# Layer 1's state from exponentials times the normalised input: two layers of conditioned attention on one core

## The chip, the core and the metric

The kernel runs on one core of a Trainium2 chip. Its engines each work through a list of instructions of their own and wait for each other by semaphores: TensorE (PE: matrix products, with its weight loads shown as PEld), VectorE (DVE), ScalarE (ACT), GpSimd (POOL) and SyncE (SP, which issues most of the transfers). The metric is the device time of one execution in microseconds, the median of several runs.

## What is computed

Two layers work on x of 2 batches x 1024 tokens x 256 channels. Layer 0 is softmax attention over the tokens with 16 heads of 16 channels; layer 1 is linear attention with 8 heads of 32 channels. Layer 1, which the change touches, is:

```
xn = _ln(x, ln_w, ln_b)
q = xn @ Wq + bq
k = xn @ Wk + bk + (1.0 - src_mask) * -1000000.0
q = softmax(q.reshape(b, t, h, dh), axis=-1)
k = softmax(k.reshape(b, t, h, dh), axis=1)
v = ((xn @ Wv + bv) * src_mask).reshape(b, t, h, dh)
att = einsum('bnhd,bnhl->bhdl', k, v)
y = einsum('bnhd,bhdl->bnhl', q, att).reshape(b, t, d)
scale, shift = split((silu(emb) @ W_emb + b_emb)[:, None, :], 2, axis=2)
hh = _ln(y, ln2_w, ln2_b) * (1.0 + scale) + shift
return x + silu(hh) @ W_out + b_out
```

`att` is the state: one 32 x 32 block per head. It is a sum over all tokens, so it needs the keys' softmax of the whole sequence, and every output needs it.

## The kernel before

Tokens are taken in 8 tiles of 128 (`NT`), channels in 2 chunks of 128 (`KC`), halves of 512 tokens (`HALF`). All engines run lists that the Python code fixes ahead.

**The main loop** is 128 steps (`STEPS`) of layer 0's attention: 16 groups (2 batches, 2 halves, 4 groups of 4 heads), each with 8 key tiles. In a step PE computes the scores of 128 keys by 512 queries for 4 heads (`scores`, L986), ACT takes their exponentials (`exponential`, L815), PE multiplies the probabilities of the step before by the values (`values`, L1006), and PE and DVE work ahead on the row maxima of later groups (L876, one product of 512 columns each; L1179, one reduction each). The maxima go round three PSUM banks (`B8[5:8]`) and, in steps that carry a large unit, also borrow banks of the scores (`sT`).

**Everything else is a "unit"**: a piece of PE work that fills one bank, which ACT or DVE then empties. `put` gives units to steps; a unit named in `SMALL` may share a step with another, any other takes a step for itself, and `places` then gives that step 5 maxima in place of 3 (the total of maxima is fixed, so a step that takes fewer leaves them to later steps). PE fills the units at the end of the step (`pe_at`), ACT empties those in `ON_ACT` after its two exponentials, DVE the others. PE waits for a bank until the unit that held it before is emptied.

Layer 1 of batch 0 runs inside the loop, of batch 1 partly. Its units:

- `("T", "in1", b, h, kc)`: `z`, the normalised input before weight and bias, transposed on PE; ACT writes `hT = ln_w * z^T + ln_b` (L904, L738).
- `keys` (L942, bias and mask by DVE, then the maximum and, on ACT, `kexp`: `kE = exp(k - max)` with its sum in `ksum`), `queries` (L851, L853; DVE subtracts the maximum, ACT takes `qexp`, DVE sums in `qsum`), `values` (`by_rows`, L851 twice 2 products and L853 twice a product that adds the bias; ACT writes `v1`, scaled by the mask, L764).
- `kT`: 4 units of 4 transposes of `kE` (L952), copied by ACT to `kN` (L768). `qT`: 4 units (L957, L771).
- `att`, one unit for each 128 channels: 8 products of `kN` by `v1` over the token tiles (L963). DVE scales by the reciprocal of `ksum` and keeps the blocks of the diagonal (L1258).
- `y1` (L970): `qT` by `att`; then the second norm, `T mid1` and `out1`.

A product of two f32 operands shows as two instructions in the trace, a transpose as one.

**The tail** follows the loop: batch 1's second half has its layer 0 output, its `in1` norm, `keys`, `queries` and `values`, and then the state. Its order is written out by hand: `end_order` for PE, `act_end` for ACT, `dve_end` for DVE, with 7 banks taken in turn. `keep_busy` puts products there whose result nobody reads.

`z` has one place per half; the next norm of that half may overwrite it once its last reader is through (L652, L1114). `late` is a shared stretch of memory: `v1` lies where the loop's early part keeps `parts`, the pieces that it stores by DMA.

Of the kernel before, what the change touches and what calls it, by code (L numbers as in the profile page):

```python
# [21 lines left out]
def two_layer_conditioned_attention(  # L22
# [6 lines left out]
    F32, F32R = mybir.dt.float32, mybir.dt.float32r  # L29
# [3 lines left out]
    P = 128  # L33
# [48 lines left out]
    with ctx:  # L82
# [66 lines left out]
        v1 = by_tile(late[:, 2 * TD:3 * TD])  # L149
# [45 lines left out]
        ctanh_ready, tanh_ready = sem("ctanh_ready"), sem("tanh_ready")  # L195
# [11 lines left out]
        ON_ACT = {"T", "v", "values", "kT", "qT", "emb"}  # L207
# [5 lines left out]
        SMALL = {"T", "kT", "qT", "att", "embT", "vec2"}  # L213
# [39 lines left out]
        last = put([("v", 1, s) for s in range(4)], last)  # L253
        for h in range(NH):
# [7 lines left out]
        last = put([("qT", 0, 1, kc) for kc in range(KC)], last)  # L262
        last = put([("att", 0, kc) for kc in range(KC)], last)
# [34 lines left out]
        dve_at[begins["values", 0, 3] + 2].append(("recips", 0))  # L298
# [58 lines left out]


# [28 lines left out]
        end_order += [("queries", b, s) for s in (2, 3)] + [("values", b, s) for s in (2, 3)]  # L387
        end_order += [("qT", b, 0, kc) for kc in range(KC)] + [("kT", b, i) for i in range(4)] + [("qT", b, 1, kc) for kc in range(KC)]
        end_order += [("att", b, kc) for kc in range(KC)] + [("y1", b, s) for s in range(4)]
# [4 lines left out]
        act_end += [("values", b, s) for s in (2, 3)] + [key for key in end_order if key[0] in ("qT", "kT")]  # L394
# [212 lines left out]
        def _(pool):  # L607
# [36 lines left out]
            def normalise(key):  # L644
# [7 lines left out]
                gone = unit[("T", *former, KC - 1)]  # L652
# [43 lines left out]
        def _(act):  # L696
# [11 lines left out]
            def take(key, ending=False):  # L708
# [52 lines left out]
                elif kind == "values":  # L761
# [74 lines left out]
        def _(pe):  # L836
# [19 lines left out]
            def fill(key):  # L856
# [74 lines left out]
                elif kind in ("out0", "out1"):  # L931
                    b, s = key[1:]
                    hT_there("mid0" if kind == "out0" else "mid1", b, s // 2)
                    if kind == "out0" and b == 0 and s == 0:
                        pe.wait_ge(wo_in, 16)
                        pe.wait_ge(w1_in, 16 * 4)
# [6 lines left out]
                elif kind in ("queries", "values"):  # L943
# [392 lines left out]
```

## Time and profile before

| | us |
|---|---|
| median of 3 runs (615.16 to 621.78) | 615.43 |
| the profiled execution | 610.35 |
| its span | 608.5 |
| PE busy, share of the span | 564.3, 93% |
| DVE busy | 450.8, 74% |
| ACT busy | 337.9, 56% |
| POOL busy | 76.5, 13% |

Overview in 40 equal slices of 15.2 us (digits are tenths; PEclk is the granted clock):

```profile
PE   8997989999999999999989999999889999977986
PEld 7454342333543344453334435555335443524765
DVE  6685886887688996878998989759888886314552
ACT  2433454555578754448667575665585566662530
POOL 3010145000000402000010230000422020002200
PEclk9999899999999996999999999999899999999998
```

The loop's first exponentials start at about 59 us and its last ones end at about 542 us; the tail is the rest. The span is read by PE's row: where it shows 9, the loop is paced by PE's list.

### The profile page before, as it was taken

How to read it: one execution, taken by the hardware profiler on the slowest of the kernel's cores; microseconds unless marked ns; L12 is line 12 of the kernel's file. 1: busy time of each engine (PE TensorE's matmuls, PEld its weight loads, DVE VectorE, ACT ScalarE, POOL GpSimd, SP SyncE). 2: the span in 40 equal slices, each digit the busy share in tenths (PEclk: the TensorE clock that was granted, in tenths of full speed). 3: DMA queues.
4: the chain of work that ended last, by engine and by line, in shares of the span. 5: the costliest groups of instructions: out<-in, count | busy, mean ns of one | idle time of the engine just before them, and what ended most of it. 6: DMA issues, size and time to landing. Idle time of an engine off the chain costs nothing. (4 is left out here: it accounts for less than half of the span.)

```text
span 608.5 us, 8404 instructions
## 1 busy us (share of the span) xinstructions
PE 564.3 (93%) x3072; PEld 273.3 (45%) x3072; DVE 450.8 (74%) x915; ACT 337.9 (56%) x410; POOL 76.5 (13%) x126
## 2 busy tenths in 40 slices
PE   8997989999999999999989999999889999977986
PEld 7454342333543344453334435555335443524765
DVE  6685886887688996878998989759888886314552
ACT  2433454555578754448667575665585566662530
POOL 3010145000000402000010230000422020002200
PEclk9999899999999996999999999999899999999998
DMA  5375991356401040404031010010002100000002
GB/s 134 93 155 115 262 236 32 83 141 149 104 27 28 2 81 0 82 0 82 14 69 28 1 28 0 2 53 15 22 2 63 34 2 2 1 0 0 1 2 69
DMA packets 18579, 33.74 MB, mean 55 GB/s; under 512 B 3930, under 2 KB 10450, under 8 KB 17772
## 3 DMA queue, kind: packets, MB, share of 16 engines
q1 hardware_dynamic: 18412, 33.17, 22.3%
q8 instruction: 25, 0.41, 0.3%
q14 instruction: 14, 0.11, 0.1%
q10 hardware_dynamic: 128, 0.04, 0.0%
HBM read 19.29 MB, written 13.52 MB: 54 GB/s over the span
## 5 line engine op out<-in xcount | busy, mean ns | idle before, releaser
L815 ACT ACTIVATE prob<-sT 128x1024 f32<-128x1024 f32 x256 | 247.7, 1023 | 122.9 <-PE sT L986 122.4
L1179 DVE TENSOR_REDUCE halfmax<-bank 128x1 f32<-128x512 f32 x424 | 268.3, 683 | 59.1 <-PE bank L876 57.5
L876 PE MATMUL bank<-ks,qs 50*128 50x512 f32 x424 | 154.3, 481 | 16.0 <-DVE halfmax L1179 8.5
L1006 PE MATMUL bank<-prob,vp 128*17 128x512 f32 x1024 | 136.8, 606 | 0.6 <-ACT prob L815 0.6
L876 PEld LDWEIGHTS bank<-ks,qs 50*128 50x128 f32 x424 | 63.2, 186 | 128.8 <-DVE halfmax L1179 76.6
L986 PE MATMUL sT<-qs,ks 52*128 52x512 f32 x512 | 106.6, 426 | 4.9 <-DMA qs<-crows 2.5
L642 POOL TENSOR_TENSOR rstd<-var,neghalf 128x4 f32<-128x4 f32 x14 | 14.2, 1015 | 483.3 <-DVE var L1103 483.3
L986 PEld LDWEIGHTS sT<-qs,ks 52*128 52x128 f32 x512 | 54.5, 189 | 21.1 <-ACT prob L815 11.3
L1179 DVE TENSOR_REDUCE halfmax<-sT 128x1 f32<-128x512 f32 x88 | 56.8, 685 | 8.0 <-PE sT L876 6.9
L851 PE MATMUL bank<-w,hT 128*128 128x256 f32 x152 | 38.7, 388 | 1.2 <-ACT hT L738 1.2
L1006 PEld LDWEIGHTS bank<-prob,vp 128*17 128x17 f32 x1024 | 17.0, 95 | 40.1 <-issue 37.4
L851 PEld LDWEIGHTS bank<-w,hT 128*128 128x128 f32 x152 | 26.5, 190 | 9.0 <-issue 4.8
L876 PEld LDWEIGHTS sT<-ks,qs 50*128 50x128 f32 x88 | 8.2, 183 | 37.5 <-ACT prob L815 37.5
L667 POOL TENSOR_TENSOR xs<-xs,bias_rows 128x256 f32<-128x256 f32 x32 | 23.3, 728 | 7.2 <-DMA bias_rows<-in_L_cond_b_out 3.2
L876 PE MATMUL sT<-ks,qs 50*128 50x512 f32 x88 | 22.0, 495 | 0.4 <-ACT prob L815 0.4
L911 PE MATMUL bank<-hT,wqk 128*128 128x512 f32 x36 | 19.3, 662 | 0.2 <-DVE halfmax L1179 0.2
L904 PE MATMUL bank<-ident,z 128*128 128x128 f32 x96 | 15.3, 295 | 4.3 <-DVE z L1120 2.4
L1199 DVE RECIPROCAL rden<-bank 128x16 f32<-128x16 f32 x16 | 4.0, 251 | 19.9 <-PE bank L899 19.9
L745 ACT ACTIVATE late<-bank,cols 128x512 fp32r<-128x512 f32 x9 | 6.2, 687 | 21.4 <-PE bank L911 21.4
L738 ACT ACTIVATE hT<-bank,cols 128x512 f32<-128x512 f32 x12 | 8.9, 774 | 14.8 <-PE bank L904 14.6
L853 PE MATMUL bank<-brow,ones 128*128 128x256 f32 x36 | 16.8, 468 | 0.0
L738 ACT ACTIVATE hT<-bank,modB,modA 128x512 f32<-128x512 f32 x12 | 9.1, 776 | 13.6 <-PE bank L904 13.2
(169 smaller groups left out, 541.8 us busy)
## 6 DMA issues: line engine op xcount, KB each, us to landing
stack_rows<-late SPq DMA_DIRECT2D x12, 512.0 KB, 6.7
qs<-stack_rows SPq DMA_DIRECT2D x30, 192.0 KB, 3.5
ks<-stack_rows SPq DMA_DIRECT2D x14, 384.0 KB
stack_rows<-late SPq DMA_DIRECT2D x17, 256.0 KB, 5.6
out_x<-xs SPq DMA_DIRECT2D x4, 512.0 KB, 2.9
xs<-in_x SPq DMA_DIRECT2D x4, 256.0 KB, 3.4
xs<-in_x SPq DMA_DIRECT2D x2, 512.0 KB, 4.0
late<-in_L_cond_emb_w SPq DMA_DIRECT2D x1, 1024.0 KB, 9.8
```

The costliest lines, as they stand in the source:

```text
L642: pool.tensor_tensor(rstd[:, L, :], var[:, L, :], neghalf[:, :], op=ALU.pow).then_inc(pow_ready, 1)
L667: pool.tensor_tensor(xs[:, t, :], xs[:, t, :], bias_rows[:, row, :], op=ALU.add).then_inc(biased, 1)
L738: act.activation(hT[:, kc, h * HALF:(h + 1) * HALF], u.bank, func, scale=scale, bias=bias).then_inc(u.done, 1)
L815: act.activation(prob[:, c % 2, 2 * u:2 * u + 2, :].rearrange("p j n -> p (j n)"), sT[u][:, :], ACT.Exp).then_inc(exp_done, 1)
L851: last = pe.matmul(o[:, i * D:(i + 1) * D], hT[:, kc, tokens], w[:, kc, :], start=(kc == 0), stop=(kc == KC - 1 and row is None))
L853: last = pe.matmul(o[:, i * D:(i + 1) * D], ones[:, :], brow[:, row, :], start=False, stop=True)
L876: last = pe.matmul(o, qs[rows, s % SLOTS, c, t * P:(t + 1) * P], ks[rows, hg, c, half * HALF:(half + 1) * HALF], start=True, stop=True)
L904: last = pe.transpose(o[:, i * P:(i + 1) * P], z[:, h * QT + i, kc * P:(kc + 1) * P], ident[:, :])
L911: last = pe.matmul(o, wqk[:, kc, hg, :], hT[:, kc, n * HALF:(n + 1) * HALF], start=(kc == 0), stop=(kc == KC - 1))
L986: last = pe.matmul(sT[u][:, two * HALF:(two + 1) * HALF], ks[rows, hg, u, c * P:(c + 1) * P], qs[rows, s % SLOTS, u, :], start=True, stop= ...
L1006: last = pe.matmul(acc[32 * j:32 * j + VW, :], vp[:, b, c, hg * GH + j, :], prob[:, c % 2, 2 * u + two, :], start=(c == 0), stop=(c == NT ...
L1179: dve.tensor_reduce(halfmax[:, s % 2, r, half:half + 1], o, axis=AX.X, op=ALU.max, negate=True).then_inc(u.done, 1)
```

## The change

The state is written another way. With E the keys' exponentials and `xn = ln_w * z + ln_b`, the sum over tokens of E times (xn @ Wv + bv) is (E^T z) scaled by `ln_w`, times Wv, plus a rank-one term: the column sums of E times the row `ln_b @ Wv + bv`. So:

- The `values` units go (4 a batch: 6 in the loop, 2 in the tail), and `v1` with them.
- New `kz` units, 2 a batch: for each 128 channels of `z`, 8 products over the token tiles with `z` as weights and 256 columns of `kN` moving; ACT writes them out scaled by `ln_w`.
- A new unit `bvb`, once, in step 26: the row `ln_b @ Wv + bv` on all partitions, copied by ACT after a wait for the last of `parts`' stores.
- `kT` is emptied with the mask as scale, in two ACT instructions of 256 columns where there was one of 512.
- `att` becomes 8 products of `kN` by one column of ones (the column sums), then 2 products of `kz` by Wv. DVE takes three chained instructions for it where it took one.
- In the tail the keys are transposed ahead of the queries, on PE and ACT; ACT empties `kz` ahead of the second half's `qT`.
- `z` is now also read by `kz`: the norm that overwrites it waits for that (`z_read`).

```diff
-        v1 = by_tile(late[:, 2 * TD:3 * TD])
+        kz = late[:, 2 * TD:2 * TD + KC * D].rearrange("p (k n) -> p k n", k=KC)
+        bvb = late[:, 2 * TD + KC * D:2 * TD + (KC + 1) * D]
+        att_sum = late[:, 2 * TD + (KC + 1) * D:2 * TD + (KC + 2) * D].rearrange("p (k n) -> p k n", k=KC)
...
-            first = put([("queries", b, 2 * h + i) for i in range(2)], first)
-            return put([("values", b, 2 * h + i) for i in range(2)], first)
+            return put([("queries", b, 2 * h + i) for i in range(2)], first)
...
+        put([("bvb",)], last + 2)
...
+        last = put([("kz", 0, kc) for kc in range(KC)], last)
         last = put([("att", 0, kc) for kc in range(KC)], last)
...
+        def z_read(key):
+            return unit["kz", key[1], KC - 1] if key[0] == "in1" else unit[("T", *key, KC - 1)]
...
-        act_end += [("values", b, s) for s in (2, 3)] + [key for key in end_order if key[0] in ("qT", "kT")]
+        act_end += [("kT", b, i) for i in range(4)] + [("qT", b, 0, kc) for kc in range(KC)]
+        act_end += [("kz", b, kc) for kc in range(KC)] + [("qT", b, 1, kc) for kc in range(KC)]
...
+                elif kind == "kz":
+                    act.activation(kz[:, key[2], :], u.bank[:, 0:D], ACT.Copy, scale=col("ln_w", key[2])).then_inc(u.done, 1)
+                elif kind == "kT":
                     for i in range(2):
                         t = 2 * key[2] + i
-                        last = act.activation(v1[:, t, :], u.bank[:, i * D:(i + 1) * D], ACT.Copy, scale=col("mask1", b * NT + t))
+                        last = act.activation(kN[:, t, :], u.bank[:, i * D:(i + 1) * D], ACT.Copy, scale=col("mask1", b * NT + t))
...
+                elif kind == "bvb":
+                    pe.wait_ge(w1_in, 16 * 4)
+                    pe.wait_ge(cols_ready, 2)
+                    for kc in range(KC):
+                        c = COL["ln_b"] + kc
+                        pe.matmul(o[:, 0:D], cols[:, c:c + 1].to_broadcast([P, P]), w1[:, 2, kc, :], start=(kc == 0), stop=False)
+                    last = pe.matmul(o[:, 0:D], ones[:, :], brow[:, 2, :], start=False, stop=True)
...
                     for t in range(NT):
-                        last = pe.matmul(o[:, 0:P], kN[:, t, kc * P:(kc + 1) * P], v1[:, t, kc * P:(kc + 1) * P], start=(t == 0), stop=(t == NT - 1))
+                        pe.matmul(o[:, P:P + 1], kN[:, t, chunk], ones[:, 0:1].bitcast(F32), start=(t == 0), stop=(t == NT - 1))
+                    pe.wait_ge(unit["kz", b, KC - 1].done, unit["kz", b, KC - 1].done_at)
+                    for i in range(KC):
+                        last = pe.matmul(o[:, 0:P], kz[:, i, chunk], w1[:, 2, i, chunk], start=(i == 0), stop=(i == KC - 1))
+                elif kind == "kz":
+                    b, kc = key[1:]
+                    for t in range(NT):
...
+                        last = pe.matmul(o[:, 0:D], z[:, t, kc * P:(kc + 1) * P], kN[:, t, :], start=(t == 0), stop=(t == NT - 1))
...
+                    dve.tensor_copy(ksum[:, b, kc:kc + 1], o[:, P:P + 1]).then_inc(ks_ready, 1)
+                    dve.wait_ge(ks_ready, 2 * (KC * b + kc) + 1)
+                    dve.scalar_tensor_tensor(out=att_sum[:, kc, :], in0=bvb[:, kc * P:(kc + 1) * P], scalar=ksum[:, b, kc:kc + 1], in1=o[:, 0:P],
+                                             op0=ALU.mult, op1=ALU.add).then_inc(ks_ready, 1)
+                    dve.wait_ge(ks_ready, 2 * (KC * b + kc) + 2)
+                    dve.scalar_tensor_tensor(out=att[:, b, kc, :], in0=att_sum[:, kc, :], scalar=rksum[:, b, kc:kc + 1], in1=blocks[:, :],
                                              op0=ALU.mult, op1=ALU.mult).then_inc(u.done, 1)
```

PE's list of the tail, from the last two products of `queries` of the kernel before (first two lines) over `values`, `qT` (L957), `kT` (L952) and `att` (L963) to `y1` (L970):

```order
L851 MATMUL sT<-w,hT 128x256 x2
L853 MATMUL sT<-brow,ones 128x256
...
L851 MATMUL bank<-w,hT 128x256 x2
L853 MATMUL bank<-brow,ones 128x256
L957 MATMUL bank<-ident,late 128x128 x8
L952 MATMUL sT<-ident,late 128x128 x16
L957 MATMUL bank<-ident,late 128x128 x8
L963 MATMUL bank<-late 128x128 x8
L963 MATMUL sT<-late 128x128 x8
L970 MATMUL sT<-att,late 128x128 x12
```

and now the same stretch behind `queries`: `kT` (L970), `qT` (L975), `kz` (L990), and for each of the two `att` units the ones (L980) and Wv (L983), then `y1` (L997):

```order
L970 MATMUL sT<-ident,late 128x128 x4
L970 MATMUL bank<-ident,late 128x128 x12
L975 MATMUL sT<-ident,late 128x128 x16
L990 MATMUL bank<-late,z 128x256 x16
L980 MATMUL bank<-ones,late 128x1 x8
L983 MATMUL bank<-w,late 128x128 x2
L980 MATMUL sT<-ones,late 128x1 x8
L983 MATMUL sT<-w,late 128x128 x2
L997 MATMUL sT<-att,late 128x128 x12
```

What moved: the four `values` groups and the 16 products of `att` are gone, all transposes stand together, and `kz` stands between them and the state.

PE's list in the loop where batch 0's state is made, before (steps 88 to 91; L876 are maxima, L986 scores, L1006 probabilities times values, L899 an output's transposes, L957 `qT`, L963 `att`):

```order
L957 MATMUL bank<-ident,late 128x128 x8
L876 MATMUL bank<-ks,qs 128x512 x2
L986 MATMUL sT<-qs,ks 128x512 x4
L1006 MATMUL bank<-prob,vp 17x512 x4
L876 MATMUL bank<-ks,qs 128x512
L899 MATMUL bank<-ident,yT 128x128 x4
L963 MATMUL bank<-late 128x128 x8
L876 MATMUL bank<-ks,qs 128x512 x2
L986 MATMUL sT<-qs,ks 128x512 x4
L876 MATMUL bank<-ks,qs 128x512
L1006 MATMUL bank<-prob,vp 17x512 x4
L963 MATMUL bank<-late 128x128 x8
```

and now, from the second `kz` unit (L990) of step 89 to the end of step 90 (the same operations are L889, L1013, L1033, L912 here):

```order
L889 MATMUL sT<-ks,qs 128x512 x2
L912 MATMUL bank<-ident,yT 128x128 x4
L990 MATMUL bank<-late,z 128x256 x8
L889 MATMUL bank<-ks,qs 128x512 x2
L1013 MATMUL sT<-qs,ks 128x512 x4
L1033 MATMUL bank<-prob,vp 17x512 x4
L889 MATMUL bank<-ks,qs 128x512
L980 MATMUL bank<-ones,late 128x1 x8
L983 MATMUL bank<-w,late 128x128 x2
L980 MATMUL bank<-ones,late 128x1 x8
L983 MATMUL bank<-w,late 128x128 x2
```

What moved: steps 88 and 89 carry one `kz` unit each, and both `att` units stand in step 90, where each had a step of its own. Between steps 50 and 90 these plans changed, no other: `values` left steps 51, 52, 83 and 84 (whose maxima went from 5 to 3), steps 58 and 59 went from 3 maxima to 5, so did 88 and 89, and the transposes moved up by one to three steps. Steps 121 and 122 lost their `values` units and carry no maxima in either kernel.

## Rows read from the trace of the kernel before

**Rows 1.** Page, busy time; and a window of 50 us (columns: stretch, length, busy, clock, DMA)

```profile
PE 564.3 (93%) x3072; PEld 273.3 (45%) x3072; DVE 450.8 (74%) x915; ACT 337.9 (56%) x410; POOL 76.5 (13%) x126
300.00:350.00 50.00, 45.46 (x273) 19.39 (x273) 45.08 (x93) 31.10 (x35) 7.41 (x13) 1.00 0.15 34
```

**Rows 2.** Timeline of ACT, steps 51 to 54 (start, us, instruction, idle before)

```profile
263.64 1.94 ACT L815 ACTIVATE prob<-sT 128x1024 f32<-128x1024 f32 x2 [3.12 <-PE sT L986]
...
269.28 1.94 ACT L815 ACTIVATE prob<-sT 128x1024 f32<-128x1024 f32 x2
...
274.28 1.94 ACT L815 ACTIVATE prob<-sT 128x1024 f32<-128x1024 f32 x2
276.64 1.94 ACT L815 ACTIVATE prob<-sT 128x1024 f32<-128x1024 f32 x2 [0.42 <-PE sT L986]
```

**Rows 3.** Timeline of PE at the start of step 51

```profile
264.45 0.50 PE L876 MATMUL bank<-ks,qs 50*128 50x512 f32 x1 [0.61 <-DVE late L1250]
```

**Rows 4.** Timeline of ACT, a step with 5 maxima and no unit

```profile
292.39 1.94 ACT L815 ACTIVATE prob<-sT 128x1024 f32<-128x1024 f32 x2 [0.52 <-PE sT L986]
296.03 1.94 ACT L815 ACTIVATE prob<-sT 128x1024 f32<-128x1024 f32 x2 [1.70 <-PE sT L986]
```

**Rows 5.** Timeline of ACT, steps 89 to 91: the two that carried `att`

```profile
400.42 1.94 ACT L815 ACTIVATE prob<-sT 128x1024 f32<-128x1024 f32 x2 [0.34 <-PE sT L986]
405.10 1.94 ACT L815 ACTIVATE prob<-sT 128x1024 f32<-128x1024 f32 x2 [2.74 <-PE sT L986]
409.19 1.94 ACT L815 ACTIVATE prob<-sT 128x1024 f32<-128x1024 f32 x2 [2.16 <-PE sT L986]
```

**Rows 6.** Timeline of ACT, steps 121 to 123, which carry no maxima

```profile
523.23 1.94 ACT L815 ACTIVATE prob<-sT 128x1024 f32<-128x1024 f32 x2 [0.87 <-PE sT L986]
...
527.73 1.94 ACT L815 ACTIVATE prob<-sT 128x1024 f32<-128x1024 f32 x2
...
531.53 3.77 ACT L815 ACTIVATE prob<-sT 128x1024 f32<-128x1024 f32 x4
```

**Rows 7.** The chain that ended last: `queries`' last bias, `values`' first products (start, us)

```profile
571.43 0.12 PE sT L853
571.55 0.86 PE sT L851 x4
```

**Rows 8.** Timeline of PE in the tail

```profile
576.18 1.91 PE L952 MATMUL sT<-ident,late 128*128 128x128 f32 x16
...
579.37 2.02 PE L963 MATMUL bank<-late 128*128 128x128 f32 x16 [0.40 <-ACT late L768]
581.22 1.95 PE L963 MATMUL sT<-late 128*128 128x128 f32 x16
583.71 2.92 PE L970 MATMUL sT<-att,late 128*128 128x128 f32 x24 [0.54 <-DVE att L1258]
```

**Rows 9.** Timeline of ACT in the tail: the first `values` unit emptied

```profile
573.63 0.82 ACT L764 ACTIVATE late<-sT,cols 128x256 f32<-128x256 f32 x2
```

**Rows 10.** Timeline of DVE: the one instruction of the state in the tail

```profile
583.21 0.35 DVE L1258 SCALAR_TENSOR_TENSOR att<-sT,rksum,blocks 128x128 f32<-128x128 f32 x1 [1.44 <-PE sT L963]
```

**Rows 11.** Two lines' instructions: f32 products of one moving column; transposes of two

```profile
L1025 PE MATMUL bank<-ident,late x12: 245/245/266, 6.2 to 7.5; 1*128 1x1 f32 x12
L930 PE MATMUL bank<-ident,late x8: 196/197/218, 115.0 to 115.4; 2*128 2x2 f32 x8
```

**Rows 12.** Windows of the tail (columns as in rows 1; the clock is third from the end)

```profile
560.00:562.00 2.00, 1.09 (x8) 0.86 (x8) 0.00 (x0) 1.27 (x2) 1.73 (x3) 1.00 0.00 0
...
564.00:566.00 2.00, 2.00 (x4) 0.89 (x3) 0.11 (x1) 0.00 (x0) 1.76 (x4) 0.54 0.00 0
...
576.00:578.00 2.00, 2.00 (x21) 2.00 (x19) 0.00 (x0) 2.00 (x5) 0.00 (x0) 1.00 0.00 0
```

**Rows 13.** Timeline of PE in the tail: `keys`, 4 instructions at a lower clock, then 4

```profile
562.23 3.62 PE L942 MATMUL bank<-hT,w 128*128 128x512 f32 x4 [1.10 <-ACT hT L738]
565.64 1.98 PE L942 MATMUL sT<-hT,w 128*128 128x512 f32 x4
```

More of the change, by code:

```diff
@@ L204, in two_layer_conditioned_attention @@
         stack_rows = nc.dram_tensor("stack_rows", [G, P, PIECES, T], F32, kind="Internal").ap()
-        ON_ACT = {"T", "v", "values", "kT", "qT", "emb"}
+        ON_ACT = {"T", "v", "bvb", "kz", "kT", "qT", "emb"}
         stream = [("max", s, m) for s in range(SUBS) for m in range(MAXES)]
-        SMALL = {"T", "kT", "qT", "att", "embT", "vec2"}
+        SMALL = {"T", "kT", "qT", "att", "embT", "vec2", "bvb"}
         at = {}
@@ L297, in two_layer_conditioned_attention @@
             dve_mid[2 * h + 2].append(("aggr", "in0", 1, h))
-        dve_at[begins["values", 0, 3] + 2].append(("recips", 0))
+        dve_at[begins["queries", 0, 3] + 3].append(("recips", 0))
         for (kind, b, h), k in layer_at.items():
@@ L386, in two_layer_conditioned_attention @@
         end_order += [("T", "in1", b, 1, kc) for kc in range(KC)] + [("keys", b, 1, kc) for kc in range(KC)]
-        end_order += [("queries", b, s) for s in (2, 3)] + [("values", b, s) for s in (2, 3)]
-        end_order += [("qT", b, 0, kc) for kc in range(KC)] + [("kT", b, i) for i in range(4)] + [("qT", b, 1, kc) for kc in range(KC)]
-        end_order += [("att", b, kc) for kc in range(KC)] + [("y1", b, s) for s in range(4)]
+        end_order += [("queries", b, s) for s in (2, 3)]
+        end_order += [("kT", b, i) for i in range(4)] + [("qT", b, 0, kc) for kc in range(KC)] + [("qT", b, 1, kc) for kc in range(KC)]
+        end_order += [("kz", b, kc) for kc in range(KC)] + [("att", b, kc) for kc in range(KC)] + [("y1", b, s) for s in range(4)]
         for h in range(NH):
@@ L942, in fill @@
                         last = pe.matmul(o, w1[:, 1, k, kc * P:(kc + 1) * P], hT[:, k, n * HALF:(n + 1) * HALF], start=(k == 0), stop=(k == KC - 1))
-                elif kind in ("queries", "values"):
-                    b, s = key[1:]
-                    last = by_rows(o, w1[:, 0] if kind == "queries" else w1[:, 2], s, 1 if kind == "queries" else 2)
+                elif kind == "queries":
+                    last = by_rows(o, w1[:, 0], key[2], 1)
+                elif kind == "bvb":
+                    pe.wait_ge(w1_in, 16 * 4)
[4 more added lines that the diff above has]
+                    last = pe.matmul(o[:, 0:D], ones[:, :], brow[:, 2, :], start=False, stop=True)
                 elif kind == "kT":
@@ L1257, in take @@
                         dve.wait_ge(blocks_ready, 1 + P // DH1)
-                    dve.scalar_tensor_tensor(out=att[:, b, kc, :], in0=o[:, 0:P], scalar=rksum[:, b, kc:kc + 1], in1=blocks[:, :],
+                    if b == 0 and kc == 0:
+                        there = unit["bvb",]
+                        dve.wait_ge(there.done, there.done_at)
+                    dve.tensor_copy(ksum[:, b, kc:kc + 1], o[:, P:P + 1]).then_inc(ks_ready, 1)
[4 more added lines that the diff above has]
+                    dve.scalar_tensor_tensor(out=att[:, b, kc, :], in0=att_sum[:, kc, :], scalar=rksum[:, b, kc:kc + 1], in1=blocks[:, :],
                                              op0=ALU.mult, op1=ALU.mult).then_inc(u.done, 1)
```

20 lines of the change are left out of this document (10 added, 10 removed).

## The prediction

> **What bounds the kernel now.** I read the page first, for busy time: PE is busy 564.3 of 608.5 us and no other engine over 451 [rows 1]. Shares are means, so the timelines come next. In the loop one step lasts from one pair of exponentials (ACT, L815) to the next, and ACT, idle before most of them, waits there for PE's scores. Step 53, which carries nothing but 3 maxima, lasts 276.64 - 274.28 = 2.36 us; step 52, with a `values` unit and 5 maxima, 274.28 - 269.28 = 5.00; step 51 before it, the same but behind `queries`, 269.28 - 263.64 = 5.64 [rows 2]. Where a step has 5 maxima and no unit, the step lasts 296.03 - 292.39 = 3.64 and ACT idles 1.70 of it [rows 4]; DVE, which must reduce them, is busy 45.1 of the 50 us that follow soon after [rows 1]. So PE's list paces steps with units, and DVE's those where postponed maxima are made up. Without maxima ACT is the bound: in step 123 and 124 four exponentials take 3.77, or 1.88 a step [rows 6]. In the tail the timelines of PE, ACT and DVE show one chain: `queries`, `values`, transposes, `att`, DVE's scaling, `y1` [rows 7, 8, 10]. All that is changed lies on PE's list or on this chain, so I cost it place by place.
>
> **The prices.** Two f32 products of 256 columns, four instructions, take 0.86 us and the bias product 0.12 [rows 7], so a `values` unit, twice that, is 1.96, and one f32 product of 256 columns is 0.43. A `kz` unit is 8 such products, 3.44. Sixteen instructions of `att`, 128 columns wide, take 581.22 - 579.37 = 1.85 [rows 8], 0.115 each, and so 8 old products are 1.85 and the 2 new ones with Wv 0.46. A transpose is at most 1.91 / 16 = 0.12 [rows 8]; the last one's latency is in that, so I take 0.11 in a row.
>
> **The ones.** 8 products by one column are 16 instructions, each with 128 columns of weights to load. What is their pitch? The nearest row is an f32 product of 128 weight columns by one moving column: 12 in 7.5 - 6.2 = 1.3 us, eleven spacings, 0.118 each. The other side is the transposes with two moving columns, 8 in 0.4, 0.057 each; they are single instructions, not pairs [rows 11]. I take 0.112, between the first and the 0.115 of `att`, for the operand types and the pairs of instructions are those of the first. The ones then cost 1.79 a unit, what the 128-column products cost: shrinking the moving side buys nothing where the weights have to be loaded anyway. `att` is 2.25 a unit in place of 1.85. At 0.057 it would be 1.37.
> The Trainium skill, page TensorE: Matmul & The Clock Gate, section Back-to-back issue gap, gives 1 to 64 moving columns a gap of about 25 ns; by that the ones would be 0.4 us a unit, an estimate from the page, and the whole sum 5.6 us lower. The products of the startup, at 0.118 [rows 11], contradict it for this form.
>
> **bvb, step 26.** Two 256-column products and a bias product, 0.99, in a step that PE paces, its eviction behind ACT's exponentials, the transfers it waits for long landed: **+1.0**. Fully hidden would be 0.
>
> **Steps 51 to 59.** The two `values` units go. Step 52 falls from 5.00 to a quiet 2.36: -2.64. Step 51 falls less far, since DVE has `queries` in hand until 264.45 [rows 3]: from there 0.43 for the probabilities' start (264.88), 0.85 for them, two maxima and scores, 0.85, and the exponentials begin near 266.8, 3.2 after 263.64: -2.4. The two `qT` transposes only change steps. Steps 58 and 59 now take 5 maxima: 2 x (3.64 - 2.36) = +2.6, DVE-bound. Sum **-2.5**. Bounds: PE's own saving, 2 x 1.96 = -3.9; and 0 if DVE takes all.
>
> **Steps 83 to 90.** Again -5.0 for the two `values` steps (same pattern, half 1). A `kz` step is a `values` step with 3.44 in place of 1.96, 6.48, against the quiet 2.36: +4.1, twice, 8.2. The `att` units cost 2 x 2.25 in place of 2 x 1.85, +0.8 (before, the two steps took 4.68 and 4.09 [rows 5]). ACT empties `kT` in two instructions of about 0.41 (two take 0.82 [rows 9]), beside exponentials of 1.94 in steps of 3.5, +0.2. DVE's three instructions follow while PE goes on with maxima: 0. Sum **+4.2**. By PE's list alone, with the old `att` as cover for nothing: -3.9 + 6.9 + 0.8 = +3.8.
>
> **Steps 121 and 122.** They last 527.73 - 523.23 = 4.50 and 3.80 [rows 6]. Without the unit ACT paces them: 1.88, and in 121 the queries' exponential, 0.6, on top: 2.5 and 1.95. Sum **-3.8**. Nothing is postponed here.
>
> **The tail.** `queries` ends at 571.55 [rows 7]. Before, `y1` began at 583.71 [rows 8]. Now:
> - 8 units of transposes on PE. `kT` takes 1.75. ACT comes to it only when the queries' exponentials are through, 573.63 [rows 9], and empties eight pieces of 0.41: 576.9. The fourth `qT` unit needs the bank of `kT` 0 (emptied 574.45) and ends at 574.9; the first `kz` needs the bank of `kT` 1, 575.3.
> - `kz`: 575.35 + 6.88 = 582.2. Its last tiles want `kT` 3 (576.9) at 577.9: no wait.
> - The ones of `att` 0, 1.79, cover ACT's emptying of `kz` 1 (0.45); Wv 0.46; `att` 1 2.25: 586.7.
> - DVE: a copy of one column, not in the trace, costs between nothing and the 0.35 of a 128-column instruction: I take 0.2; two instructions of 0.35 [rows 10], two more waits of about 0.04, and the 0.15 from the old one's end, 583.56, to `y1` at 583.71: 1.14 behind the last product where 0.52 stood. `y1` at 587.8. The second half's `qT` is emptied by ACT at 583.7, in time.
>
> **+4.1**, and what follows `y1` is unchanged.
>
> **Sum.** 1.0 - 2.5 + 4.2 - 3.8 + 4.1 = +3.0 on the profiled 610.35, whose span is 608.5. The runs' median, 615.43, lies 5.1 above the profiled one; I put the sum on it: **618.4 us**. Batch by batch: the loop's PE work falls, but `kz` gathers for the whole sequence after the keys, so what was spread over both halves' steps lands behind the wait in the tail.
>
> **Clock.** The granted clock falls to half after thin stretches: PE busy 1.09 of 2 us in 560 to 562, 0.54 granted in 564 to 566 [rows 12], and the first four instructions of `keys` take 3.62 where the next four take 1.98, less 0.2 of the last one's latency [rows 13]: +1.84 for one such stretch. The tail now has 3.5 us of nothing but transposes, then 1.79 of one-column products twice and 1.1 of idleness. Transposes alone are harmless: 576 to 578 has nothing else and is granted 1.00 [rows 12].
> The Trainium skill (TensorE: Matmul & The Clock Gate, Part 4: PE-mode transpose) says that transposes do not count as PE being busy. By that the clock should have fallen in this stretch, and `kz` would now begin at 1.2 GHz; rival 5 has the price. The row of 576 to 578 does not bear it out.
> No row shows a run of one-column products near other work.
>
> **Rivals.**
> 1. *The ones are cheap* (pitch 0.057): 32 of them a batch save 1.76, twice 3.5: **614.9**. For: the transposes of two columns. Against: the startup's products at 0.118. The 25 ns of the Trainium skill (same page and section as above) would put this rival further down still.
> 2. *The ones starve the clock*: PE counts as idle in them, and one stretch at 1.2 GHz, the lower level, follows in the loop (step 90 or 91) and one in the tail (`y1`): 2 x 1.84, **622.1**, slower than before by 1.1%. One stretch alone gives 620.2 and decides nothing; the second decides. For: 1.79 + 0.46 + 1.79 + 0.46 + 1.1 us thinly filled. Against: the tail's `att` unit before kept 1.00, and the loads of weights run on.
> 3. *DVE takes it all in steps 51 to 59*: postponed maxima cost what `values` saved: **620.9**. For: 45.1 of 50 us busy.
> 4. *The made-up maxima find gaps*: the steps made up cost only PE's price, 0.43 for two of them, and DVE fits them in: -3.9 + 0.9 in place of -2.5: **617.9**, and 617.0 if they are free.
> 5. *The transposes starve the clock*: one stretch at 1.2 GHz at the tail's first `kz`, 1.84: **620.2**. Against: 1.00 granted in 576 to 578 [rows 12]. The Trainium skill's rule on transposes, named above, is what speaks for it.
>
> **How the numbers follow.** Forecast 0.48; rival 1 0.14; rival 2 0.13; rival 3 0.10; rival 4 0.09; rival 5 0.03; something that I don't see 0.03. A change under 1%, 6.2 us, can hardly be told from none here (the three runs alone span 6.6). Forecast and rivals 1, 3, 4 and 5 lie within it: 0.84. Slower is rival 2, 0.13; faster by 1% would need 609.3, 9 us under the sum, and gets what I don't see: 0.03. The range goes from just under rival 1 to rival 2: 614 to 622.2; more than two low stretches, and more than one term off at once, are left out. The likeliest case's own range is 616.5 to 620.5.
>
> **What would show it.** `kz` units of about 3.5 us each; the ones of one unit in 1.8; steps 121 and 122 at 2.5 and 1.95; steps 88 and 89 near 6.5; from the end of `queries` to `y1` 16.3 us where 12.2 stood; the clock at 1.00 behind the ones. The prediction fails if the ones' pitch is half of what I took, if the clock falls with them, or if runs of the new kernel fall into low-clock stretches elsewhere.

## The result and the profile after

The changed kernel takes 628.0 us (median of 5 runs, 622.5 to 630.3) where the kernel before took 619.7 beside it: ratio 1.021, 95% interval 1.015 to 1.027. The forecast was 618.4 with a range to 622.2 and 0.84 on "within 1%"; the time lies above the range, on the side that had 0.13. Ratios here leave disturbed runs out, so they need not be the quotient of the medians.

The profiled execution is the fastest, 622.48 us with a span of 620.5, against 610.35 and 608.5 before. Its page: busy time and the rows of PE and of the granted clock in 40 slices:

```profile
PE 575.1 (93%) x3077; PEld 281.2 (45%) x3077; DVE 451.8 (73%) x923; ACT 336.1 (54%) x407; POOL 76.5 (12%) x126
PE   8997899999999999999989999999899999987985
PEclk9999858999999999999999799999899999999979
```

PE is busy 10.8 us more than in [rows 1], though its instructions are as many (3077 against 3072) and the share is still 93%. The clock row shows where at least part of that is: slices with 5, 7 and 7, and two with 8, where the kernel before has 9.

**The steps, as predicted or not.** First the chip's state aside: ACT at steps 51 and 52, whose `values` units went (columns: start, us, instruction, idle before and for whom):

```profile
269.58 1.94 ACT L828 ACTIVATE prob<-sT 128x1024 f32<-128x1024 f32 x2 [3.13 <-PE sT L1013]
271.41 0.63 ACT L738 ACTIVATE late<-late 128x512 f32<-128x512 f32 x1
272.57 1.94 ACT L828 ACTIVATE prob<-sT 128x1024 f32<-128x1024 f32 x2 [0.53 <-PE sT L1013]
274.80 1.09 ACT L784 ACTIVATE late<-bank 128x512 f32<-128x512 f32 x2 [0.29 <-PE bank L975]
276.22 3.00 ACT L828 ACTIVATE prob<-sT 128x1024 f32<-128x1024 f32 x3 [0.34 <-PE sT L1013]
```

Step 51 is 272.57 - 269.58 = 2.99 us (5.64 in [rows 2]), step 52 is 276.22 - 272.57 = 3.65 (5.00). The two `qT` evictions, 1.09 us of ACT, now stand in step 52 between exponentials, but ACT still waits for PE's scores behind them (0.34): PE has the `qT` transposes in this step:

```profile
274.11 1.09 PE L975 MATMUL bank<-ident,late 128*128 128x128 f32 x8
```

In steps 121 and 122 ACT alone is left:

```profile
535.83 1.94 ACT L828 ACTIVATE prob<-sT 128x1024 f32<-128x1024 f32 x2 [0.87 <-PE sT L1013]
537.65 0.63 ACT L738 ACTIVATE late<-late 128x512 f32<-128x512 f32 x1
538.17 3.77 ACT L828 ACTIVATE prob<-sT 128x1024 f32<-128x1024 f32 x4
```

From 535.83 to 538.17 are 2.34 us (4.50 in [rows 6]). The four exponentials behind it are steps 122 and 123 back to back; 122 had 3.80 before. The tail, on PE, from the end of `queries` (578.14) to `y1` (L997):

```profile
578.14 0.60 PE L970 MATMUL sT<-ident,late 128*128 128x128 f32 x4
578.57 1.47 PE L970 MATMUL bank<-ident,late 128*128 128x128 f32 x12
579.88 2.03 PE L975 MATMUL sT<-ident,late 128*128 128x128 f32 x16
581.98 7.17 PE L990 MATMUL bank<-late,z 128*128 128x256 f32 x32
588.99 1.84 PE L980 MATMUL bank<-ones,late 128*128 128x1 f32 x16
590.70 0.69 PE L983 MATMUL bank<-w,late 128*128 128x128 f32 x4
591.22 2.20 PE L980 MATMUL sT<-ones,late 128*128 128x1 f32 x16
593.28 1.20 PE L983 MATMUL sT<-w,late 128*128 128x128 f32 x4
595.59 1.62 PE L997 MATMUL sT<-att,late 128*128 128x128 f32 x6 [1.11 <-DVE att L1293]
```

The two `kz` units take 7.17 us, 3.59 each. The first 16 instructions of ones take 1.84, 588.99 to the products with Wv at 590.70 less a latency, a pitch near 0.11. The second 16 take 2.20 and the four products behind them 1.20 instead of 0.69: the clock fell within them. DVE's three instructions, behind the last product (columns as before):

```profile
594.52 0.16 DVE L1288 COPY ksum<-sT 128x1 f32<-128x1 f32 x1 [2.17 <-PE sT L983]
594.71 0.35 DVE L1290 SCALAR_TENSOR_TENSOR late<-late,ksum,sT 128x128 f32<-128x128 f32 x1
595.10 0.35 DVE L1293 SCALAR_TENSOR_TENSOR att<-late,rksum,blocks 128x128 f32<-128x128 f32 x1
```

That is 595.59 - 594.52 = 1.07 us, against 1.14 predicted. Windows of the same execution (columns as in [rows 1]; the third from the end is the granted clock): the loop over and behind its ones (413.65 to 418.3), the tail over its first 16 instructions of ones and over the second 16 with what follows them, and one stretch in steps 76 and 77, which the change does not touch:

```profile
412.00:418.00 6.00, 6.00 (x52) 4.67 (x49) 2.71 (x6) 1.94 (x2) 0.00 (x0) 1.00 0.00 1
418.00:422.00 4.00, 4.00 (x21) 1.36 (x19) 2.71 (x6) 1.94 (x2) 0.00 (x0) 0.57 0.40 131
589.00:592.00 3.00, 3.00 (x29) 3.00 (x27) 0.51 (x2) 2.73 (x4) 0.00 (x0) 1.00 0.00 0
592.00:596.00 4.00, 2.89 (x16) 2.62 (x16) 1.21 (x4) 0.00 (x0) 0.00 (x0) 0.57 0.00 0
350.00:355.00 5.00, 4.64 (x21) 1.67 (x24) 3.77 (x7) 1.60 (x3) 4.52 (x9) 0.52 0.00 0
```

Both places with ones end in a stretch near the lower level of 1.2 GHz. Steps 76 and 77 lie in one too, where the kernel before has 1.00.

**The account by stages.** Differences to the profile of the kernel before, from the starts of ACT's exponentials. In brackets: us at the lower clock in that stage, this kernel / the kernel before. Two further columns are kernels of the experiments: all ones 128 columns wide, and no ones at all with `bvb` in step 67.

| stage | predicted | changed kernel | ones 128 wide | no ones, bvb in step 67 |
|---|---|---|---|---|
| start and steps 0 to 25, same lists | 0 | +8.3 (20.5 / 3.4) | +7.3 (23.9) | +4.7 (6.8) |
| step 26 (`bvb`) | +1.0 | +1.2 | +1.2 | 0 |
| steps 27 to 50, same lists | 0 | -3.5 (0 / 10.2) | +1.9 (13.7) | -3.5 (0) |
| steps 51 to 61 | -2.5 | -2.5 | -2.5 | -2.5 |
| steps 62 to 82, same lists (last column: and `bvb`) | 0 | +2.7 (6.8 / 0) | +2.7 (6.8) | +3.5 (6.8) |
| steps 83 to 92 | +4.2 | +5.4 (3.4 / 0) | +4.2 (0) | +0.5 (0) |
| steps 93 to 120, same lists | 0 | +1.1 (6.8 / 3.4) | +1.3 (6.8) | +1.3 (6.8) |
| steps 121 to 127 | -3.8 | -4.1 | -4.1 | -4.1 |
| tail | +4.1 | +3.6 (7.5 / 8.5) | +1.0 (0.5) | -1.8 (1.0) |

Where no stretch at the lower clock lies in or beside a step, all kernels with the same list in it give it the same length within 0.04 us, but for nine steps (31, 39, 55, 60, 68, 123 to 126), which differ by up to 0.34. So the rows of "same lists" are clock.

### The profile page after: what moved, and what is told of

Read it like the earlier page. It is cut to its first block and busy times, and to the rows that moved or that the text cites. A ratio compares the mean times of both kernels' runs of the same rounds, so it can differ in the third digit from the quotient of the medians.

```text
span 620.5 us, 8422 instructions
## 1 busy us (share of the span) xinstructions
PE 575.1 (93%) x3077; PEld 281.2 (45%) x3077; DVE 451.8 (73%) x923; ACT 336.1 (54%) x407; POOL 76.5 (12%) x126
## 5 line engine op out<-in xcount | busy, mean ns | idle before, releaser
L889 PE MATMUL bank<-ks,qs 50*128 50x512 f32 x428 | 157.3, 489 | 16.8 <-DVE halfmax L1206 9.3
L1033 PE MATMUL bank<-prob,vp 128*17 128x512 f32 x1024 | 140.5, 622 | 0.3 <-ACT prob L828 0.3
L889 PEld LDWEIGHTS bank<-ks,qs 50*128 50x128 f32 x428 | 64.7, 189 | 133.6 <-DVE halfmax L1206 77.4
L1013 PE MATMUL sT<-qs,ks 52*128 52x512 f32 x512 | 109.0, 433 | 5.9 <-DMA qs<-crows 3.5
L1013 PEld LDWEIGHTS sT<-qs,ks 52*128 52x128 f32 x512 | 55.6, 191 | 23.2 <-ACT prob L828 12.4
L1206 DVE TENSOR_REDUCE halfmax<-sT 128x1 f32<-128x512 f32 x84 | 54.0, 684 | 8.5 <-PE sT L889 7.9
L1033 PEld LDWEIGHTS bank<-prob,vp 128*17 128x17 f32 x1024 | 17.1, 96 | 40.8 <-issue 38.3
L864 PE MATMUL bank<-w,hT 128*128 128x256 f32 x96 | 24.1, 388 | 1.2 <-ACT hT L748 1.2
L889 PEld LDWEIGHTS sT<-ks,qs 50*128 50x128 f32 x84 | 7.8, 183 | 36.5 <-ACT prob L828 36.5
L889 PE MATMUL sT<-ks,qs 50*128 50x512 f32 x84 | 21.2, 501 | 0.5 <-ACT prob L828 0.5
L864 PEld LDWEIGHTS bank<-w,hT 128*128 128x128 f32 x96 | 16.9, 190 | 6.3 <-issue 3.0
L917 PEld LDWEIGHTS bank<-ident,z 128*128 128x128 f32 x96 | 11.6, 154 | 10.2 <-DVE halfmax L1206 4.3
```

The costliest lines, as they stand in the source:

```text
L864: last = pe.matmul(o[:, i * D:(i + 1) * D], hT[:, kc, tokens], w[:, kc, :], start=(kc == 0), stop=(kc == KC - 1 and row is None))
L889: last = pe.matmul(o, qs[rows, s % SLOTS, c, t * P:(t + 1) * P], ks[rows, hg, c, half * HALF:(half + 1) * HALF], start=True, stop=True)
L917: last = pe.transpose(o[:, i * P:(i + 1) * P], z[:, h * QT + i, kc * P:(kc + 1) * P], ident[:, :])
L1013: last = pe.matmul(sT[u][:, two * HALF:(two + 1) * HALF], ks[rows, hg, u, c * P:(c + 1) * P], qs[rows, s % SLOTS, u, :], start=True, stop= ...
L1033: last = pe.matmul(acc[32 * j:32 * j + VW, :], vp[:, b, c, hg * GH + j, :], prob[:, c % 2, 2 * u + two, :], start=(c == 0), stop=(c == NT ...
L1206: dve.tensor_reduce(halfmax[:, s % 2, r, half:half + 1], o, axis=AX.X, op=ALU.max, negate=True).then_inc(u.done, 1)
```

## The experiments

**The kernels themselves again.** The spread from run to run had to be known first; neither kernel has an edit.

> The kernel before, once more, to have the granted clock and the span of each of its runs beside those of the changed kernel. The profile after showed 12.0 us more in the span, of which 8.3 lie before step 26, where both kernels run the same list: 2.7 in the first 15 us, where the clock rose later, and 4.9 in steps 3 to 6, where 17 us were granted at half. Theory A (chance): the place and number of the low-clock stretches vary from run to run in either kernel, so this kernel too shows such runs: a profile with another set of stretches than 61, 231 to 241, 436, 562 and 593, runs between 610 and 622, mean granted clock between 0.955 and 0.98. Theory B (the change brings them): this kernel stays at 0.97 to 0.98 in all runs, and the same stretches as in the first profile come back.

> The changed kernel once more. The steps and the tail that the change touches account for +3.5 us in the profiles: +1.2, -2.5, +5.4, -4.1, +3.6. Theory A: the ratio to the kernel before comes down to 1.004 to 1.010, and its runs overlap with those of the kernel before; the stretches behind the ones (418 and 592) may come back or not. Theory B: the ratio stays at 1.015 to 1.025, and the mean granted clock stays 0.01 to 0.02 under that of the kernel before.

Measured: the kernel before again 617.0 us (611.2 to 623.3, 12 runs), ratio 1.005 (1.001 to 1.009), though nothing was changed: a ratio within 0.5% means nothing here. Its profile repeats that of the kernel before, low stretches included, within 0.6 us. The runs differ with their mean granted clock: 611.2 us at 0.979, 616.96 at 0.963, 623.28 at 0.955, about 4 us per 0.01. So each theory was half right: the runs spread as Theory A has it, the profile repeated as Theory B has it. The changed kernel again: 622.8 us (621.3 to 629.5, 6 runs) beside 614.05 (23 runs), ratio 1.019 (1.014 to 1.023); mean clock 0.960 against 0.971. At 4 us per 0.01 the clock is 4.4 of the 8.8 us between the medians. This is Theory B of the second text: the difference stayed. In its profile, which has a span of 627.6, the clock stays low for longer behind the ones of the loop:

```profile
418.00:423.00 5.00, 5.00 (x25) 2.32 (x24) 2.75 (x6) 1.94 (x2) 0.00 (x0) 0.58 0.33 105
423.00:429.00 6.00, 6.00 (x25) 3.12 (x25) 3.96 (x6) 1.94 (x2) 0.00 (x0) 0.50 0.00 0
```

**Ones 128 columns wide.** The same weights and the same number of products, with more for the array to do.

```diff
-pe.matmul(o[:, P:P + 1], kN[:, t, chunk], ones[:, 0:1].bitcast(F32), ...)
+pe.matmul(o[:, P:2 * P], kN[:, t, chunk], ones[:, 0:P].bitcast(F32), ...)
```

> The changed kernel, but the column sums are taken with 128 moving columns of ones in place of one (the 127 further columns of the result are not read). If the pitch of 0.112 us comes from loading 128 f32 weight columns, a product with 128 moving columns costs as much: 16 instructions in 1.8 us, units and steps as long as before. If the ones starve the clock (the stretches at 418 and 592 to 599 begin just behind them), filling the array's moving side takes both stretches away: 1.2 us less in step 91 and 2 to 2.5 less around y1 in the tail, 3 to 4 us in all. If the clock fell there by chance or for the wait of 1.1 us behind them, nothing changes.

Measured: 619.5 us (617.4 to 623.3, 6 runs), ratio 1.012 (1.008 to 1.016). Steps 83 to 92 are +4.2, as forecast, and the whole is 3.3 us under the narrow form. Windows over and behind the ones of the loop, and over and behind those of the tail:

```profile
418.00:422.00 4.00, 4.00 (x36) 3.94 (x36) 1.55 (x4) 0.47 (x1) 0.00 (x0) 1.00 0.00 2
422.00:426.00 4.00, 3.87 (x28) 1.93 (x27) 2.89 (x7) 1.94 (x2) 0.00 (x0) 1.00 0.37 131
592.00:597.00 5.00, 4.99 (x43) 4.75 (x41) 0.86 (x3) 2.73 (x4) 0.00 (x0) 1.00 0.00 0
597.00:601.00 4.00, 2.90 (x26) 2.93 (x27) 2.39 (x6) 0.00 (x0) 0.00 (x0) 1.00 0.02 4
```

The clock is 1.00 throughout. The tail's first transposes (the end of `queries`) and its `y1` on PE:

```profile
581.50 0.60 PE L970 MATMUL sT<-ident,late 128*128 128x128 f32 x4
...
598.10 2.13 PE L997 MATMUL sT<-att,late 128*128 128x128 f32 x17 [1.11 <-DVE att L1293]
```

16.6 us between them at full clock, where 16.3 were forecast and 17.45 stand in the changed kernel.

**No ones.** `att` is the product over `kz` with Wv, times the reciprocal of the keys' sum, plus `bvb`: DVE needs no sum from PE, and two instructions instead of three.

```diff
-for t in range(NT):
-    pe.matmul(o[:, P:P + 1], kN[:, t, chunk], ones[:, 0:1].bitcast(F32), ...)
-dve.tensor_copy(ksum[...], o[:, P:P + 1])
-dve.scalar_tensor_tensor(out=att_sum, in0=bvb, scalar=ksum, in1=o[:, 0:P], op0=mult, op1=add)
-dve.scalar_tensor_tensor(out=att, in0=att_sum, scalar=rksum, in1=blocks, op0=mult, op1=mult)
+dve.scalar_tensor_tensor(out=att_sum, in0=o[:, 0:P], scalar=rksum, in1=bvb, op0=mult, op1=add)
+dve.tensor_tensor(att, att_sum, blocks, op=mult)
```

> The changed kernel without the products with ones: the rank-one term is added after the scaling, att = (kz^T Wv) / ksum + bvb, which holds for masks of 0 and 1 (exponentials of masked keys are 0, so that the sums over the tokens divide out); masks between are left out. It removes 32 instructions of 0.112 us a batch, 3.6 in step 90 and 3.6 in the tail, and DVE's copy, 0.2. By the step account it ends 7.2 to 7.5 us under the changed kernel and 3.5 to 4 under the kernel before. If the ones also starve the clock, another 3 us go, 10 to 11 in all. If, instead, the ones had been hidden behind something else, the gain is under 4.

Measured: 611.75 us (610.0 to 619.4, 12 runs), ratio 0.997 (0.993 to 1.000), 11.1 us under the changed kernel, at the upper end of the 10 to 11 expected of the clock and the steps together. Against the kernel before the ratio is no further from 1 than the unchanged kernel's own. Step 90 is 3.39 us (6.96 with wide ones, so 3.57 for the two units' ones), the tail 67.3.

**bvb alone, in the kernel before.** The edit is the change's `bvb` unit with its line in the plan, `put([("bvb",)], last + 2)`.

> The kernel before with one part of the change alone: step 26 also makes bvb (two products over the broadcast LayerNorm bias and one over the bias row), which nothing reads. Step 26 took 1.17 us longer in the changed kernel. Theory A (the parts add up, and the low clock comes from the ones): +1.2 us, ratio 1.002, mean granted clock as in the kernel before (0.971 over its 23 runs). Theory B (whatever moves the steps after 26 against the clock brings the new low stretches, of which steps 76 and 77 had one in all four changed kernels so far and in neither profile of the kernel before): one or two more low stretches, clock near 0.965, +3.5 us or more, ratio 1.006 or above, and a low stretch in steps 76 and 77.

Measured: 616.8 us (613.6 to 627.2, 12 runs), ratio 1.005 (1.001 to 1.010), as much as the unchanged kernel gave; mean clock 0.969. Step 26 is 3.46 us against 2.28, +1.18. Steps 76 and 77 are unchanged. A window of this kernel in these steps, and one of the kernel with wide ones added (below):

```profile
350.00:355.00 5.00, 4.41 (x28) 1.53 (x27) 4.41 (x8) 3.11 (x4) 4.52 (x9) 1.00 0.00 0
```

```profile
354.00:359.00 5.00, 4.64 (x20) 1.55 (x16) 3.59 (x6) 2.01 (x4) 4.52 (x9) 0.54 0.00 0
```

The second kernel has the list of the kernel before up to step 88 and fell there; the first has the shift and did not. Theory B is not borne out: the low stretch of steps 76 and 77 needs no shift. This kernel's profile does have one stretch that neither profile of the kernel before has, in steps 36 and 37 (+1.9 us in steps 27 to 50), but so has the kernel with narrow ones added, which has no shift there either. What decides from run to run whether such a stretch comes stays open.

**The ones alone, in the kernel before,** narrow and 128 wide, ahead of each `att` unit's own products:

```diff
+for t in range(NT):
+    pe.matmul(o[:, P:P + 1], kN[:, t, kc * P:(kc + 1) * P], ones[:, 0:1].bitcast(F32), ...)
```

> The kernel before, values and all, with the 16 one-column products of the change put ahead of each att unit's own products (two units in the loop, two in the tail) into columns that nobody reads. At the 0.112 us pitch 16 of them take 1.8 us: 3.6 us in the loop and 3.6 us in the tail, of which the tail shows all and the loop what PE does not wait anyway. Theory A (narrow products let the clock fall): 7.2 us of products plus a low stretch behind each pair, 1 to 3 us each: +9 to +12 us, ratio 1.015 to 1.020, and low stretches right behind the ones in the loop and in the tail. Theory B (no effect on the clock): +7.2 us, ratio 1.012, clock as in the kernel before.

> As the kernel with narrow ones added, but each of the 64 products has 128 moving columns of ones in place of one. In the changed kernel the wide ones took PE as long as the narrow ones within 0.4 us a pair. Theory A: +7.2 us, ratio 1.012, no low stretch behind the ones in the loop or in the tail, 2 to 5 us faster than with narrow ones. Theory B: the same time as with narrow ones within 1 us.

Measured: narrow 628.4 us (617.8 to 636.3), ratio 1.015 (1.005 to 1.024); wide 621.5 (620.2 to 629.3), ratio 1.017 (1.010 to 1.024), 6 runs each. The medians are 6.9 us apart, the ratios not at all: in the total this pair is inconclusive, since two narrow runs had a clock of 0.98, and the faster of them (617.8) is under every wide one. The place is clear in the profiles. PE in step 89, narrow, then wide:

```profile
407.87 1.84 PE L963 MATMUL bank<-ones,late 128*128 128x1 f32 x16
409.58 3.52 PE L965 MATMUL bank<-late 128*128 128x128 f32 x16
```

```profile
413.17 1.95 PE L963 MATMUL bank<-ones,late 128*128 128x128 f32 x16
414.96 1.95 PE L965 MATMUL bank<-late 128*128 128x128 f32 x16
```

Both forms are followed by the next products after 1.7 to 1.8 us. Behind the narrow ones the old `att` products take 3.52 us, behind the wide ones 1.95. Step 90, with a clock of 1.00 in both, is 1.79 us longer than before in either: the predicted price. The 16 narrow instructions of that step brought no low stretch of their own, so not every such row of them does.

In the tail narrow ones cost 7.3 us (17.1 us at the lower clock) and wide ones 0.3, where 3.6 were expected. Two low stretches of the kernel before's tail are missing in this profile. One lay in `keys` [rows 13], the other in an output's products (L851); first the latter in the kernel before, then both places with wide ones:

```profile
593.38 5.26 PE L851 MATMUL sT<-w,hT 128*128 128x256 f32 x16 [1.19 <-ACT hT L738]
```

```profile
577.80 1.98 PE L942 MATMUL bank<-hT,w 128*128 128x512 f32 x4 [1.10 <-ACT hT L738]
610.84 3.69 PE L851 MATMUL sT<-w,hT 128*128 128x256 f32 x16 [1.19 <-ACT hT L738]
```

That is 3.62 - 1.98 = 1.6 us and 5.26 - 3.69 = 1.6, nearly the whole 3.3 us. `keys` stands ahead of the tail's ones (593.25), so the first 1.6 is not their doing; whether the second is, one profile does not show.

**bvb in step 67,** without ones: `put([("bvb",)], 67)` in place of `put([("bvb",)], last + 2)`.

> The kernel without ones (att as the product over kz times the reciprocal of the keys' sum, plus bvb, which holds for masks of 0 and 1) with bvb made in step 67 instead of step 26. In step 67 PE waits twice for DVE's halfmax, 0.76 and 0.65 us, at full clock, where step 26 took 1.17 us longer by bvb. Theory A (those waits take bvb in, and PE has more to do where the clock often falls): 1 us or more under the kernel with bvb in step 26, so 610 to 611 us where that one had 611.75 beside a before of 614.05: ratio 0.993 to 0.996, step 67 within 0.5 us of its 4.21 us. Theory B (the bank that bvb holds delays the halfmax behind it, so the waits stay): ratio 0.997, step 67 1.2 us longer.

Measured: 608.3 us (605.1 to 618.5, 12 runs) beside 615.7 (23 runs), ratio 0.989 (0.985 to 0.992): 1.1% under the kernel before, beyond Theory A's 0.993. PE in step 67, first its last wait with `bvb` in step 26, then `bvb`'s first products here:

```profile
319.66 0.50 PE L889 MATMUL bank<-ks,qs 50*128 50x512 f32 x1 [0.65 <-DVE halfmax L1204]
```

```profile
314.85 1.13 PE L962 MATMUL bank<-w,cols 128*128 128x256 f32 x4
```

The 0.65 us wait is filled; the other, ahead of it, stays at 0.75. Step 67 is 4.81 us instead of 4.21, step 68 3.41 instead of 3.29, step 26 2.29 instead of 3.46: about 0.45 us gained, less than half of what was expected. The other 2.9 us of the 3.5 between the medians are not this mechanism: in the profile 2.7 come from steps 44 and 45, which had a low stretch in one kernel and none in the other, and the mean clock is 0.976 against 0.972.

**Ones twice,** narrow and wide, in the changed kernel, since the pairs above overlapped. The edit repeats the ones' loop into columns that nobody reads.

> The changed kernel with its one-column products made twice: 16 more of them ahead of each att unit's own, into a column that nobody reads; at the 0.112 us pitch +1.79 us a unit, 7.2 us in all for the two units of the loop and the two of the tail. The changed kernel had 622.8 us beside a before of 614.05. Theory A (one-column products let the clock fall): the clock falls within them as well as behind them, so 32 in a row are paid at the lower clock too; low stretches of 6.8 us or more at both places, step 90 and 91 together above 18 us (14.0 in the second profile of the changed kernel, plus 3.6), 633 to 638 us, ratio 1.030 or more, and 5 us or more above the wide twin. Theory B (ones cost PE's time alone): 630 us, ratio 1.025, the wide twin within 1.5 us, which has the same number of products.

> The twin: the changed kernel with its ones products made twice and each with 128 moving columns in place of one. Theory A: PE's time alone, 7.2 us over the kernel with wide ones once (619.5 us beside 614.05), 626 to 627 us, ratio 1.020 to 1.023; step 90 at 10.5 us (6.96 with wide ones once, plus 3.58), step 91 at 4.2, and no low stretch in steps 90 to 92 nor between kz and y1 in the tail. Theory B: 630 us, as the narrow twin.

Measured: narrow 639.1 us (634.3 to 646.0), ratio 1.042 (1.034 to 1.049); wide 629.6 (622.6 to 635.0), ratio 1.023 (1.016 to 1.031), 6 runs each. The intervals are apart, by 9.6 us in the medians, with the same number of products; mean clock 0.949 and 0.963. Both totals are above what was expected, the narrow one by 1 us or more, the wide one by 3: its profile has 20.5 us at the lower clock in steps 93 to 120, which no ones precede. PE at the second unit of the loop, narrow (L980 and L982 are the two loops), then wide:

```profile
413.24 3.41 PE L980 MATMUL bank<-ones,late 128*128 128x1 f32 x16
416.52 3.55 PE L982 MATMUL bank<-ones,late 128*128 128x1 f32 x16
419.93 1.20 PE L985 MATMUL bank<-w,late 128*128 128x128 f32 x4
```

```profile
415.75 1.95 PE L980 MATMUL bank<-ones,late 128*128 128x128 f32 x16
417.54 1.95 PE L982 MATMUL bank<-ones,late 128*128 128x128 f32 x16
419.32 0.61 PE L985 MATMUL bank<-w,late 128*128 128x128 f32 x4
```

Step 90 lasts 17.03 us with the narrow form and 10.53 with the wide one (predicted 10.5), and the tail 80.8 and 75.3. Over the twelve profiles, the loop's place behind the ones is at the lower clock in all four with narrow ones (the changed kernel twice, narrow ones added, narrow ones twice), and in none of the others: three with wide ones, two without ones, the kernel before (twice) and `bvb` alone. In the tail, too, the clock falls within or behind the ones in those four and in none of the three with wide ones.

## Why the prediction was wrong, by its own steps

**The steps' prices held.** At full clock the changed places sum to +3.2, forecast +3.0: step 26 +1.2, steps 51 to 61 -2.5, steps 83 to 92 +4.2, steps 121 to 127 -4.1, and from the end of `queries` to `y1` 16.6 - 12.2 = +4.4, the last and the third from the kernel with wide ones. (The tail as a whole is only +3.6 in the changed kernel, though this part is 17.45 - 12.2 = +5.3: the kernel before lost time at half clock in its `keys` [rows 13], where the changed one ran at 1.00.) The ones' pitch of 0.112 us was right in both forms wherever the clock was 1.00, so rival 1 is out: 16 narrow instructions added 1.79 us to step 90 of the kernel before, and 32 wide ones are 3.57 us of it in the changed kernel, 0.112 each. The 25 ns of the Trainium skill (TensorE: Matmul & The Clock Gate, Back-to-back issue gap) did not fit this form, and my reading of it was too short: the section calls its table the gap of an isolated product and says that at small widths it counts too little, because the loading of weights is not in it. Some parts of the sum in steps 51 to 61 were off and cancelled: step 52 fell to 3.65 instead of 2.36, because the `qT` transposes that "only change steps" now stand on PE's list there (274.11), and steps 53 and 54, which they left, fell by 0.4 and 0.6; steps 57 to 59 grew by 0.9, 1.0 and 0.8 us, not by 1.28 twice, and step 60 shrank by 0.4. Rival 3 is out, at -2.5, and so is rival 4: the made-up maxima cost 2.3 us in steps 57 to 60, not 0.9. Steps 83 to 92 came out at +4.2 by luck as well: steps 83 to 85 gave back 3.5 us and not 5.0, and steps 88 to 91 cost 7.6 with wide ones where 9.2 were summed, since steps 88 and 89 had been no quiet steps of 2.36 before (3.75 and 4.68).

**What failed is the weight on rival 2.** It said that the ones starve the clock in the loop and in the tail, at 622.1 us, and had 0.13. That is what happened, in both places. The sum itself put the clock behind the ones at nothing; narrow against wide, the clock cost 1.2 and 4.0 us in steps 83 to 92 (two profiles of the changed kernel) and 2.6 in the tail. I counted against it that "the tail's `att` unit before kept 1.00" and that "the loads of weights run on". The `att` unit was no evidence, since its products have 128 columns; and full weight loading did not keep the clock in the narrow form, as the pair of ones twice shows with the same loads. Its price was too small as well: 1.84 us for each place is one short stretch, and the second profile has one of 10.2 us in the loop. With the ones doubled, narrow against wide is 6.5 us in step 90 and 5.5 in the tail.

**Second, the comparison took the clock of the other steps as given.** The sum went on a median of three runs, 615.4; beside the changed kernel the same kernel had 619.7, and that is 4.3 of the 9.6 us by which the forecast missed. I also left "more than two low stretches" out of the range. The kernel before alone runs from 608 to 627 us, and over the twelve profiles the low stretches that come and go lie in a handful of steps whose lists never change (0 to 7, 36 and 37, 44 and 45, 67, 76 and 77, 98 to 100, 103). Of the 12.0 us between the two profiled spans, 8.6 lie in such steps and the start: +8.3 -3.5 +2.7 +1.1.

Medians of many runs even some of this out, but not all. In the profiles the changed places together differ from the kernel before by +3.6 and +7.6 us (changed kernel, two profiles), -0.2 (ones 128 wide) and -6.7 (no ones), two low stretches in the kernel before's own tail counted in; the medians differ by +8.8, +5.4 and -2.3. So 1 to 6 us of each difference come from elsewhere, from steps whose lists are the same. Steps 76 and 77 have a low stretch in six of the seven profiles of kernels with `kz` and in one of the five others: whether the change brings it there or chance does is not shown. Of the 8.8 us I can name 3.2 at full clock and some 3 behind the ones (narrow against wide: 3.3 in the medians); the rest, 2 to 3 us, stays open.

**Rival 5 is out.** The transposes in a row (578.14 to 581.9) are followed by `kz` at 0.22 us an instruction, full speed, as the row of 576 to 578 had said [rows 12]. The rule in the Trainium skill (TensorE: Matmul & The Clock Gate, Part 4: PE-mode transpose), by which `kz` should have begun at the lower level, did not decide here.

## What to carry to other kernels

Price a product by what it loads, and look at the granted clock behind it: where the weights have to be loaded, a moving side of one column costs PE what 128 columns cost, and a row of such products can cost the clock behind it too. If such a sum is needed, take it from another engine or fold it into a scale that is there already, as the reciprocal of the keys' sum was; if it must be on PE, give it the full width (128 columns for one took 6.5 us off step 90 with the ones made twice). Before small predictions are made, read the granted clock of several executions of the same kernel: here it moves the time of one kernel by up to 19 us, six times the change's own sum.

## What was not expected of the hardware

- A low stretch that happens to be missing can hide work: 32 wide instructions more in the tail, 3.6 us of PE, lengthened it by 0.3 us in one profile, since two stretches at 1.2 GHz were missing there, one of which stood ahead of the added work.
- 16 instructions of narrow ones take 1.84 us at the higher level and 3.4 to 3.6 at the lower one, and their weight loads 192 and 333 ns each.
- Most steps are repeatable to 0.04 us wherever the clock is 1.00, over twelve profiles, so that a fraction of a microsecond in one step can be read from a single execution, while 5 us in the total can't.
- At the start the same 12 one-column products take 245 ns each in the kernel before and 347 in the changed one, though the views show a granted clock of 1.00 in both. The trace's list of clock levels begins only at 6.1 us in the one and at 12.3 in the other, behind these products (6.4 to 8.7 us), and where it has no entry the views count full speed. Over the twelve profiles the loop's first exponentials start at 58.3 to 59.8 us where the list begins by 7.1, and at 62.3 to 63.6 in the three where it begins at 12.3 to 15.0. So the 3.4 us by which the start is longer in the changed kernel are probably clock too; the level before the first entry is not recorded.
